# Moving the Newton step of the queries' inverse norm from VectorE to GpSimd, and eps into a column of the squares

## The reference, cut to what matters

```python
def _qknorm(t, scale):
    norm = jax.lax.rsqrt(jnp.mean(t * t, axis=-1, keepdims=True) + EPS)
    return t * norm * scale
...
q = _qknorm(q, q_scale)       # 16 query heads of 128, EPS = 1e-06
k = _qknorm(k, k_scale)       # 4 key heads
...
scores = jnp.einsum('bhtd,bhsd->bhts', q, k) * scale
attn = jax.nn.softmax(jnp.where(causal, scores, min), axis=-1)
out = jnp.einsum('bhts,bhsd->bhtd', attn, v)
```

## Time and profile before

| | |
|---|---|
| median of 3 runs | 420.47 us (418.64 to 420.99) |
| profiled execution | 419.07 us |
| its span | 417.3 us |
| PE busy | 367.4 us (88%) |
| DVE busy | 331.4 us (79%) |
| ACT busy | 275.9 us (66%) |
| POOL busy | 218.5 us (52%) |

### The profile page before, as it was taken

The page is one execution under the profiler, slowest core; times in us unless marked ns, Lnnn a source line. Parts: engine busy times, 40 slices in busy tenths (PEclk is TensorE's granted clock), DMA queues, the critical chain, the costliest instruction groups (busy, mean ns, idle before and its releaser), DMA issues.

```text
span 417.3 us, 6425 instructions
## 1 busy us (share of the span) xinstructions
PE 367.4 (88%) x1952; PEld 294.3 (71%) x1952; DVE 331.4 (79%) x779; ACT 275.9 (66%) x673; POOL 218.5 (52%) x229
## 2 busy tenths in 40 slices
PE   0098778899999789898998987999899999999995
PEld 0097566688878667687776876687587878888884
DVE  8999788999988997789999889486557777665543
ACT  5547778798889498696976887785375434453321
POOL 7160613179524858225585121464259756888831
PEclk9999989999999999999999999999999999999999
DMA  7735300113100304001031000111065343274121
GB/s 214 297 87 183 104 0 0 52 52 102 53 0 2 102 0 137 15 3 50 2 101 40 1 2 0 38 41 38 2 160 172 138 126 81 97 218 173 53 75 50
DMA packets 14209, 31.92 MB, mean 76 GB/s; under 512 B 1872, under 2 KB 4432, under 8 KB 14176
## 3 DMA queue, kind: packets, MB, share of 16 engines
q1 hardware_dynamic: 13888, 31.38, 23.6%
q10 hardware_dynamic: 288, 0.14, 0.1%
HBM read 30.43 MB, written 1.08 MB: 76 GB/s over the span
## 4 chain that ended last, share of the span: by engine, by line
PE 53%; DVE 25%; ACT 15%; issue 5%; POOLq 0%; POOL 0%; DVEq 0%; ACTq 0%
PE ov L1223 6%; PE sc L1201 5%; PE acc L1126 4%; PE acc L1127 4%; PE acc L1128 4%; PE tr L1152 4%; ACT PR L623 4%; DVE B L868 3%; DVE F L868 3%; DVE PR L1062 3%; PE proj L1140 3%; PE tr L1128 2%; PE tr L1126 2%; PE tr L1127 2%; PE sc L1126 2%
## 5 line engine op out<-in xcount | busy, mean ns | idle before, releaser
L596 POOL TENSOR_TENSOR WL<-stage,WH 128x256 fp32r<-128x256 f32 x142 | 125.9, 916 | 75.1 <-ACT WH L662 75.1
L610 POOL TENSOR_TENSOR PR<-PR,RI 128x512 f32<-128x512 f32 x48 | 53.6, 1133 | 83.8 <-DVE RI L1072 83.8
L1140 PE MATMUL proj<-WH,RH 128*128 128x512 f32 x96 | 42.5, 443 | 33.0 <-DVE RL L921 19.9
L1126 PE MATMUL acc<-OH,WH 128*128 128x256 f32 (+1 forms) x172 | 54.5, 317 | 2.9 <-DVE OL L1084 2.2
L623 ACT ACTIVATE PR<-PR,MX 128x128 f32<-128x128 f32 (+1 forms) x128 | 56.9, 458 | 0.0
L1127 PE MATMUL acc<-OL,WH 128*128 128x256 f32 (+1 forms) x172 | 53.1, 309 | 0.0
L1128 PE MATMUL acc<-OH,WL 128*128 128x256 f32 (+1 forms) x172 | 53.0, 308 | 0.0
L1201 PEld LDWEIGHTS sc<-kT,QT 128*128 128x128 f32 x256 | 41.6, 193 | 16.1 <-issue 12.9
L1201 PE MATMUL sc<-kT,QT 128*128 128x128 f32 (+1 forms) x256 | 47.8, 330 | 0.0
L1223 PE MATMUL ov<-PTS,V 128*128 128x512 f32 x96 | 46.6, 594 | 1.1 <-DVE OL L1084 1.1
L1140 PEld LDWEIGHTS proj<-WH,RH 128*128 128x128 f32 x96 | 18.4, 192 | 39.5 <-issue 37.2
(11 more groups left out here) (160 smaller groups left out, 878.4 us busy)
## 6 DMA issues: line engine op xcount, KB each, us to landing
stage<-in_ffn SPq DMA_DIRECT2D x22, 384.0 KB, 3.3
stage<-in_wq SPq DMA_DIRECT2D x8, 512.0 KB, 3.3
stage<-in_wo SPq DMA_DIRECT2D x8, 512.0 KB, 3.4
SBC<-group_scalars SPq DMA_DIRECT2D x8, 256.0 KB, 3.6
PR<-in_tables SPq DMA_DIRECT2D x4, 352.0 KB, 7.2
fT<-in_fT SPq DMA_DIRECT2D x4, 256.0 KB, 3.8
xT<-in_xT SPq DMA_DIRECT2D x4, 256.0 KB, 4.1
stage<-in_wk SPq DMA_DIRECT2D x2, 512.0 KB, 4.7
```

Of the source, the lines that this page charges most:

```text
L596: i = pool.tensor_tensor(lo[:, c:c + 256], src[:, c:c + 256], hi[:, c:c + 256].bitcast(F32), ALU.subtract)
L610: pool.tensor_tensor(pr, pr, RI[:, m % 4, hs[0]:hs[0] + nh].rearrange("p (h o) -> p h o", o=1).broadcast_to([P, nh, 512 // nh]), ALU.mult) ...
L1126: mm(o, lh, rh, start=first, stop=False, skip_group_check=True)
L1140: mm(proj[:], rh[ch], wh[ch], start=ch == 0, stop=False, skip_group_check=True)
```

## The change

1. The squares of a head get a 129th column that holds 128 x eps. It is written once by GpSimd at the start; ACT writes the 128 squares beside it. The sum over 129 columns is then 128 x (mean + eps), and the VAR instruction and its semaphore are gone. Ln takes the sum with scale 1/128.
2. The Newton step of the queries (N) goes from DVE to GpSimd, in four small instructions with a semaphore between each and the next. It stands first in the odd iteration of GpSimd's queue, ahead of that iteration's splits and of S. The keys' Newton step (K2) stays on DVE.
3. Three places of the plan change: K3 of token tile 3 of the first half from iteration 5 to 6, and K3 of tiles 0 and 1 of the second half from 16 and 17 to 17 and 18.

```diff
     "DVE": [...
-            ("kv", 0), ("bg", 0), ("F", 6), ("N", 0), ("S", 2), ("rest", 0), ("kv", 0),
-            ("L", 5), ("C", 1)],
-    "POOL": [("bg", 0), ("S", 2), ("bg", 0), ("bg", 0), ("rest", 0)],
+            ("kv", 0), ("bg", 0), ("F", 6), ("S", 2), ("rest", 0), ("kv", 0), ("L", 5),
+            ("C", 1)],
+    "POOL": [("N", 0), ("bg", 0), ("S", 2), ("bg", 0), ("bg", 0), ("rest", 0)],
...
-    for half, places in (((0, 1), [2, 4, 4, 5, 5]), ((1, 0), [15, 15, 15, 16, 17]), ((1, 1), [17, 18, 18, 19, 19])):
+    for half, places in (((0, 1), [2, 4, 4, 5, 6]), ((1, 0), [15, 15, 15, 17, 18]), ((1, 1), [17, 18, 18, 19, 19])):
...
+            pool.memset(SQ[:, :, :, D:D + 1], D * EPS).then_inc(s["eps_ready"], 1)
...
+                elif st[0] == "N":
+                    n = NORM[st]
+                    pool.wait_ge(s["rs_act"], n + 1)
+                    y, a, b_, r, total = (x[:, n % NST, :, :] for x in (Y0, NA_, NB_, RQ, SS))
+                    linked(pool.tensor_tensor(a, y, y, ALU.mult))
+                    linked(pool.tensor_tensor(b_, a, total, ALU.mult))
+                    linked(pool.tensor_scalar(a, b_, 0.5 / D, -1.5, ALU.mult, ALU.add))
+                    pool.tensor_tensor(r, a, y, ALU.mult).then_inc(s["rq_ready"], 1)
...
-                    nc.scalar.activation(SQ[:, e % 2, :], proj[:], ACT.Square).then_inc(s["square_ready"], 1)
+                    nc.scalar.activation(SQ[:, e % 2, :, 0:D], proj[:].rearrange("p (h n) -> p h n", h=REP), ACT.Square).then_inc(s["square_ready"], 1)
...
-                    act.wait_ge(s["var_ready"], n + 1)
-                    nc.scalar.activation(LN[:, n % NST, :, :], VAR[:, n % NST, :, :], ACT.Ln).then_inc(s["act_link"], 1)
+                    act.wait_ge(s["sumsq_done"], NORM_END[n] + 1)
+                    nc.scalar.activation(LN[:, n % NST, :, :], SS[:, n % NST, :, :], ACT.Ln, scale=1.0 / D).then_inc(s["act_link"], 1)
...
-                if half_:
-                    dve.wait_ge(s["sumsq_done"], e + 1)
-                    v.tensor_scalar(VAR[:, n % NST, :, :], SS[:, n % NST, :, :], 1.0 / D, EPS, ALU.mult, ALU.add).then_inc(s["var_ready"], 1)
+                v.tensor_reduce(SS[:, n % NST, half_, :], SQ[:, e % 2, :, :], X, ALU.add).then_inc(s["sumsq_done"], 1)
...
-                linked(v.scalar_tensor_tensor(out=a, in0=y, scalar=0.5, in1=var, op0=ALU.mult, op1=ALU.mult))
+                linked(v.scalar_tensor_tensor(out=a, in0=y, scalar=0.5 / D, in1=total, op0=ALU.mult, op1=ALU.mult))
...
-                elif st[0] == "N":
-                    refine(st)
```

More of the change, by code:

```diff
@@ L263 @@
                                       if q[-1] % 2])}
+NORM_END = [e for q, e in TOK.items() if q[-1] % 2]
 ND = {1: 17, 2: 16}
@@ L371, in program @@
         QT = sb("QT", [P, 3, REP, P])
-        SQ = sb("SQ", [P, 2, REP * D])
+        SQ = sb("SQ", [P, 2, REP, D + 1])
         NST = 4
-        SS, VAR, LN, Y0, NA_, NB_, RQ = (sb(n, [P, NST, 2, REP]) for n in ("SS", "VAR", "LN", "Y0", "NA_", "NB_", "RQ"))
+        SS, LN, Y0, NA_, NB_, RQ = (sb(n, [P, NST, 2, REP]) for n in ("SS", "LN", "Y0", "NA_", "NB_", "RQ"))
         MX, RS, RI = (sb(n, [P, 4, REP]) for n in ("MX", "RS", "RI"))
@@ L426, in program @@
         wkv_act wkv_dve tanh1_done r1_ready r2_ready tanh2_done base_gated rh2_done
-        proj_full tr_full tok_ready square_ready sumsq_done var_ready rs_act rq_ready kn_ready q_turned k_turned v_ready table_full tables_cleared table_hi table_lo
+        proj_full tr_full tok_ready square_ready sumsq_done eps_ready rs_act rq_ready kn_ready q_turned k_turned v_ready table_full tables_cleared table_hi table_lo
         scores_full max_ready exp_done rinv_ready p_ready pt_act pt_dve ov_full o_hi o_lo wo_done x1_ready
@@ L926, in sum_squares @@
                 dve.wait_ge(s["square_ready"], e + 1)
-                v.tensor_reduce(SS[:, n % NST, half_, :], SQ[:, e % 2, :].rearrange("p (h n) -> p h n", h=REP), X,
-                                ALU.add).then_inc(s["sumsq_done"], 1)
-                if half_:
-                    dve.wait_ge(s["sumsq_done"], e + 1)
-                    v.tensor_scalar(VAR[:, n % NST, :, :], SS[:, n % NST, :, :], 1.0 / D, EPS, ALU.mult, ALU.add).then_inc(s["var_ready"], 1)
+                if e == 0:
+                    dve.wait_ge(s["eps_ready"], 1)
+                v.tensor_reduce(SS[:, n % NST, half_, :], SQ[:, e % 2, :, :], X, ALU.add).then_inc(s["sumsq_done"], 1)
             def refine(st):
@@ L936, in refine @@
                 dve.wait_ge(s["rs_act"], n + 1)
-                y, a, b_, r, var = (x[:, n % NST, :, :] for x in (Y0, NA_, NB_, RQ, VAR))
-                linked(v.scalar_tensor_tensor(out=a, in0=y, scalar=0.5, in1=var, op0=ALU.mult, op1=ALU.mult))
+                y, a, b_, r, total = (x[:, n % NST, :, :] for x in (Y0, NA_, NB_, RQ, SS))
+                linked(v.scalar_tensor_tensor(out=a, in0=y, scalar=0.5 / D, in1=total, op0=ALU.mult, op1=ALU.mult))
                 linked(v.tensor_tensor(b_, a, y, ALU.mult))
```

## The result

The kernel after takes 421.38 us (median of 11 runs, 421.14 to 423.35), the kernel before 419.08 us (median of 11, 418.43 to 421.01). The ratio is 1.0059, with a 95% interval of 1.0037 to 1.0081: 2.3 us slower, just over the 0.5% that can be told from no change. The time lies inside the predicted range (413.5 to 423.0), but the range was wide enough for either sign: the likeliest case was 417.1, faster than before, and the kernel became slower. That it lies inside is luck. The case that came about is the first rival, "GpSimd's order eats it". The 1.40 us that the prediction added for the median of the runs came from three runs only: over eleven the median of before is 419.08, and its profiled execution took 419.07. From there the sum of -3.4 us leads to 415.7, so the working was off by 5.7 us.

What follows compares the result with a forecast made beforehand. No engine bounds the whole: PE does from 77 to 124 us, DVE from 178 to 260. The terms, -3.4 us against 419.07, give 415.7; with 1.40 for the median of runs 417.1 us, 80% range 413.5 to 423.

Steps and rivals of the forecast that it cites:

- GpSimd's order eats it: Rival: late or displaced splits on GpSimd cost more than the gains; 420.5 us in the middle, 418.5 to 422.5, chance 0.27.
- The 1.40 us that the prediction added: Offset of the median of runs above the profiled execution, taking the forecast from 415.7 to 417.1 us.
- VAR and N off DVE: Removing the VAR instruction and Newton steps from DVE's queue saves 3.9 us, bounds 2 and 5.
- sum over 129 columns: DVE's sum of squares, with 4 more elements each, costs 0.2 us over 40 sums.
- GpSimd's chain: Four small Newton instructions on GpSimd take 1.0 us, just fit the 1.1 us from Y to C, and cost 0.
- split of iteration 9: On GpSimd it now runs after N, ends late, and PE waits 1.8 us at item 10's projection; range 1.0 to 3.3.
- split of iteration 5: On GpSimd it moves beside two-input WKV steps: 1.2 us more on DVE, half absorbed, so 0.6 us.
- splits of iteration 23: Two splits and S follow each other on GpSimd; iteration 25's output weights come barely in time: 0.3 us, up to 1.
- K3 moves: PE and DVE waits around K3 in iterations 5 and 16 go: 1.4 plus 1.0, 2.4 us gained, bounds 0.5 and 3.
- the second of the two things the prediction named as proof against it: Sign of a wrong prediction: DVE's saved time turns up as idle time before OL and the squares.

Runs made afterwards that it cites:

- e2: Kernel after with the queries' Newton step N back on DVE, eps column and moved K3 steps kept: 415.95 us, ratio 0.9913.
- e3: Kernel before with the three moved K3 steps alone, no eps column, N on DVE: 417.88 us, ratio 0.9960.
- e5: e1 with DVE making RQ, while GpSimd runs its four Newton instructions into tiles nobody reads: 417.98 us, ratio 0.9975.
- e7: e2 with the queries' Newton step left out of every engine, the scores taking Y0: 414.65 us, ratio 0.9885.
- e1: Kernel after with N behind the iteration's first split (or state clearing) on GpSimd in iterations 5, 9, 15, 17, 23: 416.80 us, ratio 0.9929.
- e4: Kernel after with N behind the split on GpSimd in iteration 9 alone: 419.72 us, ratio 1.0014.
- e11: Kernel before with the eps column alone, N on DVE and no K3 moved: 417.99 us, ratio 0.9965.
- e6: e1 with the second GpSimd Newton instruction done five times over, a chain of eight: 428.23 us, ratio 1.0201.
- e8: Kernel after with N behind the first split on GpSimd in iterations 5, 9 and 23 alone: 416.73 us, ratio 0.9934.
- e9: e2 with K3 of tile 1 of the second half in iteration 17 instead of 18: 416.69 us, ratio 0.9945.

## Why the prediction was wrong, step by step

From e2, e3, e5, e7 and the traces, each term of the sum beside what it was:

| term | forecast | measured |
|---|---|---|
| VAR and N off DVE | -3.9 | -3.3: VAR -2.0 (e2 less e3, without the next row), N -1.3 (e7 less e2) |
| sum over 129 columns | +0.2 | +0.1 (40 x 3 ns) |
| GpSimd's chain | 0 | +2.15 (e1 less e7): S held up +1.2 to +2.0 (e5 less e2, without and with the wait at 95 us), scores of the first pairs +0.4 (traces of e1 and e2) |
| split of iteration 9 | +1.8 | +1.7 (after less e4) |
| split of iteration 5 | +0.6 | +0.85 (traces of e4 and e1: 1.25 at 96 us, of which 0.4 come back by 150 us) |
| splits of iteration 23 | +0.3 | +1.4 (traces of e4 and e1), and 1.5 more where the clock falls, in that execution |
| K3 moves | -2.4 | -1.2 (e3) |
| sum | -3.4 | +1.7 (medians: +2.3) |

By these rows the splits make 3.95 us; measured together (after less e1) they make 4.6, and the 0.6 us between the two is what the rows do not place. The terms -1.3 and +2.15 give the 0.85 us of e1 less e2. The term of VAR is that beside the K3 moves; alone it was 1.0 (e11), which stays open.

- **N and VAR off DVE**: too high by 0.6 us. The idle time in front of OL rose from 6.3 us in before to 17.1 in after, while with N on DVE (e2) it is 7.7: much of the time that DVE was saved turned into waiting for OH, the second of the two things the prediction named as proof against it. The groups of OL in before and e2:

```profile
L1084 DVE TENSOR_TENSOR OL<-ov,OH 128x512 fp32r<-128x512 f32 x32 | 21.6, 675 | 6.3 <-ACT OH L787 6.2
```

```profile
L1092 DVE TENSOR_TENSOR OL<-ov,OH 128x512 fp32r<-128x512 f32 x32 | 21.6, 675 | 7.7 <-ACT OH L797 7.6
```

- **The chain costs 0**: the failed step, and the largest one. Its length was right (101.63 to 102.68, 1.05 us against an estimated 1.0; from start to start an instruction takes 0.28 us, 0.08 of it the step to the next, where 0.06 was taken, a figure that no run shows), and C waits for RQ in few pairs: 4.0 us of idle time in two, both among the first, which other idle time absorbs but for 0.4. What failed is the price of what stands behind N in GpSimd's queue. The prediction put S behind N, but asked only who reads it: PE's D, two iterations later. It did not ask which DVE step S then lies beside. In e1 RI is ready at 244.91 and S starts at 246.14, where in e2 it starts with RI, and the WKV product beside it is longer. By e1 less e7 the chain cost 2.15 us against the 1.3 us that N gave on DVE. So N on GpSimd loses even where no split is late. An order with S ahead of N was not run; S takes 2.04 us, and e6, where RQ came only some 1.15 us later, lost 11.4 us, so it is not likely to gain.
- **The split of iteration 9**: right in place, size and mechanism.
- **The split of iteration 5**: the mechanism was right, the size too small: 1.25 us where it arises, 0.85 in the end. The WKV steps beside it in after and before, DVE timeline:

```profile
73.59 0.79 DVE L903 TENSOR_TENSOR F<-F,B 128x512 f32<-128x512 f32 x1
74.31 1.23 DVE L905 TENSOR_TENSOR EU<-EUX,fT 128x512 f32<-128x512 f32 x1
75.47 1.21 DVE L907 TENSOR_TENSOR F<-F,EUX 128x512 f32<-128x512 f32 x1
76.71 1.15 DVE L909 TENSOR_SCALAR F<-F 128x512 f32<-128x512 f32 x1
77.78 1.53 DVE L912 TENSOR_TENSOR F<-F,B 128x512 f32<-128x512 f32 x1
```

```profile
75.90 1.02 DVE L893 TENSOR_TENSOR F<-F,B 128x512 f32<-128x512 f32 x1
76.84 0.68 DVE L895 TENSOR_TENSOR EU<-EUX,fT 128x512 f32<-128x512 f32 x1
77.44 0.68 DVE L897 TENSOR_TENSOR F<-F,EUX 128x512 f32<-128x512 f32 x1
78.16 0.43 DVE L899 TENSOR_SCALAR F<-F 128x512 f32<-128x512 f32 x1
78.50 0.69 DVE L902 TENSOR_TENSOR F<-F,B 128x512 f32<-128x512 f32 x1
```

  Five steps take 5.91 instead of 3.50 us: the split, and behind it S, which now reaches to 78.76. Even the tensor_scalar L909, with one input, takes 1.15 us for 0.43. The prediction took 1.2 us for these steps and half of it as absorbed; they take 2.4 us more, and PE is 1.25 us later in e4 than in e1 by item 9.
- **The splits of iteration 23**: the wrong consumer. The forecast looked at when the output weights are ready (they were in time) and not at the WKV steps of iteration 24 beside the late split. These took 1.35 us longer, the output product that reads OL of item 19 started 1.4 us later, and this is where the clock fell.
- **The K3 moves**: both gains were found (1.7 and 1.0 us), but the moved step was not charged where it went: a wait of 0.54 us and twice its own 0.4 us on a PE that is the bound there. The prediction said that K3 "costs later" and gave it no number.

The rival "GpSimd's order eats it" said 420.5 in the middle and named the three splits' costs, though not S behind N. It got 0.27 because only one displaced split has a reader in the next iteration. Readers were not the only ones to ask about.

## What to carry to other kernels

Before a waiting step goes to the head of an in-order queue, write down for every place what stands behind it and what each of those now lies beside: lateness can cost through a reader, or through a neighbour on another engine with which it then contends. A step that stands in the shade of a wait is worth little where it is (here 1.3 us for 16 x 3 x 0.166 = 8 us of busy time), so price the whole removal first by a run that leaves it out. And when a step is moved off a stall, charge its own duration again at the new place.

## What the runs showed that was not expected

PE's clock has a share in the result. Windows of after around the output product of iteration 25:

```profile
227.00:229.50 2.50, 1.01 (x6) 0.42 (x4) 2.46 (x5) 2.31 (x5) 0.40 (x2) 1.00 0.50 145
229.50:233.30 3.80, 3.50 (x17) 3.53 (x18) 3.44 (x14) 2.38 (x10) 0.93 (x3) 0.56 0.04 12
233.30:234.50 1.20, 1.20 (x10) 1.14 (x10) 0.00 (x0) 0.00 (x0) 1.03 (x4) 0.98 0.00 0
```

PE was busy for 1.01 of 2.50 us, waiting for OL, and then the granted clock lay at its lower level, 1.2 GHz, for most of 3.8 us. The output product, whose 24 matmuls take 3.0 us from first start to last end in before, took 4.6. From PE's timeline of after, at the lower and at the higher level:

```profile
231.12 0.41 PE L1132 MATMUL acc<-OH,WH 128*128 128x256 f32 x1
...
233.88 0.28 PE L1132 MATMUL acc<-OH,WH 128*128 128x256 f32 x1
```

In before, PE runs into the same product at full clock, and in e1 and e2 too. The runs of after lie in two groups, 421.1 to 421.8 (7) and 422.6 to 423.4 (4), those of e4 at 419.1 to 419.9 (7) and 420.9 to 421.4 (5), and both profiled executions, with the fall in them, belong to the upper groups. That the lower groups had no fall there fits, but only one execution of each was profiled. The mean granted clock of every run does not settle it: one fall of 3.4 us in 421 makes 0.996, and in after ten of the eleven runs have 0.996, in both groups, so the lower ones had a fall too, perhaps at a place where it costs nothing. In e4 five of the seven lower runs have 1.0, and all five upper ones 0.992 or 0.996. The runs of before lie in two groups as well, 418.4 to 419.1 (6) and 420.5 to 421.0 (5), and after is about 2.5 us slower in either.

A fall does not cost time everywhere. The clock also fell in before, e1, e7, e8 and e9 from about 58 to 62 us, and not in after, e2, e3, e4 and e5, after nearly the same idle time (2.13 us in e1, 2.14 in e4, before the same matmul). Windows of before and of after:

```profile
59.00:62.00 3.00, 3.00 (x9) 2.33 (x7) 2.34 (x8) 2.42 (x7) 0.48 (x1) 0.50 0.00 0
```

```profile
59.00:62.00 3.00, 2.07 (x10) 1.47 (x8) 2.38 (x8) 2.88 (x8) 0.24 (x1) 1.00 0.00 0
```

There it cost nothing: e1 and e4, alike up to there but for the fall, start the next transposes at 63 us within 0.02 us of each other.
